# Two moves in the matmul engine's order of a fused attention and feed-forward block

## The reference, cut to what matters

```python
x = x + tanh(g_xattn) * attention(layernorm(x), ctx, ctx, mask, Wq, bq, Wk, bk, Wv, bv, Wo, bo)
x = x + tanh(g_ffn) * ffn(layernorm(x))

def ffn(h):
    h = qat_lora_linear(h, W_fc, b_fc, A_fc, B_fc)          # 256 -> 1024
    h = gelu(h)                                             # exact
    return qat_lora_linear(h, W_proj, b_proj, A_proj, B_proj)   # 1024 -> 256

def qat_lora_linear(x, W, b, A, B):
    scale = max(abs(W)) / 127                               # one scale for the whole matrix
    Wq = clip(round(W / scale), -128, 127) * scale
    return x @ Wq.T + b + 2.0 * (x @ A.T) @ B.T             # rank 16
```

## Time and profile before

| | |
|---|---|
| median of 3 runs | 204.48 us (203.13 to 204.89) |
| profiled execution | 204.89 us, span from first to last instruction 202.9 us |
| PE, PEld | 187.9 us (93%), 140.4 us (69%) |
| DVE | 145.4 us (72%) |
| ACT, POOL | 107.2 us (53%), 108.2 us (53%) |
| mean granted TensorE clock | 0.98 of full |

### The profile page before, as it was taken

The page is one execution under the profiler, slowest core; times in us unless marked ns, Lnnn a source line. Parts: engine busy times, 40 slices in busy tenths (PEclk is TensorE's granted clock), DMA queues, the critical chain, the costliest instruction groups (busy, mean ns, idle before and its releaser), DMA issues.

```text
span 202.9 us, 3501 instructions
## 1 busy us (share of the span) xinstructions
PE 187.9 (93%) x1241; PEld 140.4 (69%) x1241; DVE 145.4 (72%) x295; ACT 107.2 (53%) x187; POOL 108.2 (53%) x145
## 2 busy tenths in 40 slices
PE   6999965999996999999999999999998989999992
PEld 4656832566775976786778856967787748867991
DVE  2869799678289478897568979776479865954724
ACT  3151935784857446665447356643465464236521
POOL 3528979236939548539249662185377640344600
PEclk9999998799999799999999999999999999999998
DMA  6997000000060000000000000000000000010002
GB/s 182 262 251 277 22 0 2 5 0 0 2 210 0 0 0 29 0 27 29 26 0 0 3 0 26 29 26 26 0 2 5 0 29 26 0 52 3 0 0 103
DMA packets 10010, 8.38 MB, mean 41 GB/s; under 512 B 3165, under 2 KB 9722, under 8 KB 9994
## 3 DMA queue, kind: packets, MB, share of 16 engines
q1 hardware_dynamic: 9538, 8.03, 12.4%
q10 hardware_dynamic: 456, 0.14, 0.4%
HBM read 6.07 MB, written 2.10 MB: 40 GB/s over the span
## 4 chain that ended last, share of the span: by engine, by line
PE 72%; POOL 9%; DVE 8%; issue 6%; ACT 4%; DVEq 0%; POOLq 0%
PE ps L1190 13%; PE ps L1170 6%; PE ps L1114 6%; PE ps L1144 6%; PE ps L1103 6%; PE ps L1174 6%; POOL shifted L316 5%; PE ps L987 4%; PE ps L1124 4%; PE ps L1131 4%; PE ps L1212 2%; PE ps L1181 2%; PE ps L978 2%; PE ps L1158 2%; ACT probsT L447 2%
## 5 line engine op out<-in xcount | busy, mean ns | idle before, releaser
L316 POOL TENSOR_TENSOR shifted<-shifted,row_max 128x512 f32<-128x512 f32 x32 | 35.8, 1133 | 17.3 <-DVE row_max L752 17.2
L1190 PE MATMUL ps<-wprojT,h_hi 128*128 128x288 f32 x128 | 37.2, 314 | 1.7 <-ACT wprojT L496 1.7
L803 DVE TENSOR_TENSOR h_lo<-wfc_sb,h_hi 128x512 fp32r<-128x512 f32 x32 | 25.3, 797 | 17.4 <-POOL h_hi L335 17.4
L1190 PE MATMUL ps<-wprojT,h_lo 128*128 128x288 f32 x128 | 35.6, 301 | 0.0
L335 POOL TENSOR_SCALAR h_hi<-wfc_sb 128x512 fp32r<-128x512 f32 x32 | 21.9, 689 | 23.9 <-ACT wfc_sb L632 23.9
L632 ACT ACTIVATE wfc_sb<-ps,bias_cols,wscale 128x512 f32<-128x512 f32 x32 | 24.5, 779 | 18.8 <-PE ps L1181 16.9
L1190 PEld LDWEIGHTS ps<-wprojT,h_hi 128*128 128x128 f32 x128 | 24.9, 195 | 2.8 <-ACT wprojT L496 2.2
L447 ACT ACTIVATE probsT<-ps 128x512 f32<-128x512 f32 x32 | 19.0, 598 | 14.2 <-PE ps L1114 13.9
L739 DVE TENSOR_TENSOR shifted<-ps,mask_neg 128x512 f32<-128x512 f32 x32 | 20.8, 683 | 7.4 <-PE ps L1103 7.2
L1190 PEld LDWEIGHTS ps<-wprojT,h_lo 128*128 128x128 f32 x128 | 24.8, 194 | 0.2
L1114 PE MATMUL ps<-ident,shifted 128*128 128x128 f32 x128 | 20.2, 284 | 4.2 <-POOL shifted L316 4.2
(11 more groups left out here) (154 smaller groups left out, 375.7 us busy)
## 6 DMA issues: line engine op xcount, KB each, us to landing
wfc_sb<-in_L_ffn_W_fc SPq DMA_DIRECT2D x1, 1024.0 KB, 7.6
wproj_sb<-in_L_ffn_W_proj SPq DMA_DIRECT2D x1, 1024.0 KB, 8.9
wproj_sb<-in_x SPq DMA_DIRECT2D x2, 512.0 KB, 3.8
out<-x_front SPq DMA_DIRECT2D x8, 128.0 KB, 1.7
out<-wproj_sb SPq DMA_DIRECT2D x8, 128.0 KB, 1.7
x_front<-in_x SPq DMA_DIRECT2D x2, 256.0 KB, 3.6
x_front<-in_x SPq DMA_DIRECT2D x1, 512.0 KB, 4.6
wk_sb<-in_L_xattn_Wk SPq DMA_DIRECT2D x1, 256.0 KB, 3.9
```

The lines of the kernel that those rows point to most:

```text
L316: nc.gpsimd.tensor_tensor(shifted[:, slot], shifted[:, slot], row_max[:, slot].unsqueeze(2).broadcast_to([P, HH, KC]), ALU.subtract)\
L803: nc.vector.tensor_tensor(h_lo[:, f], hidden[:, f % HIDDEN_SLOTS], h_hi[:, f].bitcast(F32), ALU.subtract).then_inc(h_split, 1)
L1190: last = nc.tensor.matmul(dst[:, 0:DOWN], h[:, f, t * P:(t + 1) * P], wprojT[:, f], start=(f == 0 and n == 0), stop=(f == FC - 1 and n == ...
```

## The change

The transposes of W_proj's first half move from behind up tile 5 to behind up tile 4 (after the lora product of tile 2). ACT reads them behind gelu 5 in place of gelu 6. The scores of the next chunk's second pair leave the loop over up tiles (they stood behind tile 7) and become the first work of `attention_start`, behind the last lora product; in chunk 1's case they also stand behind the wait for the read of W_proj's first half. The scores of the first pair stay behind tile 3. All other queues keep their order.

```diff
-SCORED = (3, 7)
...
-                    if c == 0 and f == 6:
+                    if c == 0 and f == 5:
                         read_wprojT(0)
...
-                    if c == 0 and f == 5:
+                    if c == 0 and f == 4:
                         transpose_wproj(0)
-                    if c < LAST and f in SCORED:
-                        scores(c + 1, SCORED.index(f))
+                    if c < LAST and f == 3:
+                        scores(c + 1, 0)
                     if c == 0 and f == 7:
                         transpose_wproj(1)
...
                 if c == 1:
                     wait_read(pe, ("wprojT", 0))
                     pe.wait_ge(aT_ready, 1)
+                scores(c, 1)
                 down(c - 1, 0, 0)
```

## The result

| | before | after |
|---|---|---|
| median of 10 runs | 204.38 us (202.82 to 205.08) | 201.64 us (200.40 to 203.15) |
| profiled execution | 204.89 us, span 202.9 | 201.03 us, span 199.0 |
| mean granted clock in that execution | 0.98 | 0.996 |

After to before is 0.9881 (by the means, 201.59 to 204.01), with a 95% interval of 0.9834 to 0.9929: faster, by 1.2%. The forecast was 202.3, with 200.8 to 204.1.

The account below looks back on a forecast made before the run. TensorE, busy 93% of the span, was taken as the bound; its wait for W_proj's read cost twice, by length and slow clock. 204.89 - 0.84 - 1.55 = 202.50, or 202.09 against the median; forecast 202.3, range 200.8 to 204.1 us.

Parts of the forecast that it names:

- (a): Chunk 0, up tile 4: moved W_proj transposes cost PE nothing; following POOL and DVE work up to 0.43 us later.
- (b): First boundary: W_proj read behind gelu 5 starts at 61.20, ends 62.21; PE resumes 0.26 us later, at 62.47.
- (c): First boundary: PE's wait 0.92 us in place of 1.75, first down product 0.84 earlier; later boundaries 0.
- (d): Behind the first boundary's wait: the slow clock stretch goes, gain 1.55 us.
- (e): After the first down products: second shift still in time by 0.27 us; bound 0 to 0.44, taken as 0.
- the slower rival: All three boundaries: POOL and DVE contention lengthens two shifts by 0.43 each, 2.6 us in all; 206.6 us, chance 0.06.
- Only the shorter wait counts: First boundary: slow stretch stays, gain only 0.84; 203.6 us against the median, 204.0 against the profiled execution; chance 0.27.
- Both slow stretches go: Boundary's slow stretch and the untouched one at 34 to 38 both absent: 200.9 us, chance 0.15.

Follow-up runs that it names:

- the first kernel with only the other stops filled: Kernel before, unread 128-column matmuls filling PE's four stops in chunk 0's attention, boundary wait unfilled: ratio 0.9985; medians 201.83 us at whole clock, 203.12 with one slow stretch.

## Why the prediction was right

**(a) The transposes moved at no cost: right.** They stand behind lora 2 with no stop (the row has no bracket), and from lora 5 on the boundary has the same order of work as forecast.

```profile
54.99 0.62 PE L1062 MATMUL ps<-ident_bf,probsT 128*128 128x128 bf16 x8
```

One reading under (a) was off: 54.48 is where POOL begins its copies of gelus 0 and 1, two in 1.21 us, so the bank was free near 55.1 and not by 54.48. That was still some 1.2 ahead of the transposes.

**(b) The read behind gelu 5: right, and mis-sized in one term.** Gelu to read is 0.68 again. But PE goes on 0.05 after the read's end (60.89 to 60.94), where 0.26 was taken over from the old profile. With late scores alone it is 0.06 (61.40 to 61.46). Where a down product comes first it is 0.26 before, 0.25 and 0.26 with the wait filled, and 0.35 in the first kernel with only the other stops filled (63.10 to 63.45).

```profile
60.39 1.01 ACT L495 ACTIVATE wprojT<-ps 128x1024 fp32r<-128x1024 bf16 x1
62.09 1.01 ACT L496 ACTIVATE wprojT<-ps 128x1024 fp32r<-128x1024 bf16 x1
```

The first row is of the late scores, the second of that kernel. So the delay goes with what stands first behind the wait; I had put it down to the wait. What in the down product takes the 0.2 to 0.3 was not tried.

**(c) The stop: right.** 0.80 against a forecast of 0.92, and the first down product earlier by 1.03 against 0.84; that difference of 0.19 is the 0.21 of (b) but for 0.02. At the later boundaries the forecast of 0 holds. From the fourth pair's scores of the first boundary to those of the second it was 42.87 before,

```profile
73.08 0.39 PE L1103 MATMUL ps<-k_hi,q_hi 64*128 64x256 f32 x2
...
115.95 0.39 PE L1103 MATMUL ps<-k_hi,q_hi 64*128 64x256 f32 x2
```

and it is 42.86 after (69.17 to 112.03); from the second to the third it was 42.96 (115.95 to 158.91) and is 42.98 (112.03 to 155.01).

```profile
69.17 0.39 PE L1102 MATMUL ps<-k_hi,q_hi 64*128 64x256 f32 x2
...
107.17 0.66 PE L1113 MATMUL ps<-ident,shifted 128*128 128x128 f32 x4 [0.43 <-POOL shifted L315]
...
112.03 0.39 PE L1102 MATMUL ps<-k_hi,q_hi 64*128 64x256 f32 x2
```

The stop of 0.43 for the second shift is that of the earlier trace rows; the rows are of the changed kernel.

**(d) The clock: right in direction and price, wrong as a certainty.** The price, 1.55, was measured as 1.54 in the profiled pair and as 1.3 to 1.4 between the levels of the kernel with its other stops filled. But the forecast took it as lost in every run before and won in every run after. With the other stops filled it was lost in 5 of 12 at this stop, and in 0 of 12 after. The reason given for its going, a stop shorter than the 1.55 at 27.76 that left the clock at 1.00, was weak: stops of 1.5 and 1.84 at the boundary also leave the clock whole in some runs. What the comparison of medians shows, 2.74, is 1.0 of shorter stop, and the rest goes with fewer slow stretches; in the profiled pair one of the two that are gone is that at 34, which the change leaves alone. That the forecast's 2.39 came near is in part luck: the ten runs of before have a median of 204.38, the 75 beside the experiments one of 203.37, only 1.7 above the changed kernel.

**(e) What is late next: right.** No stop for a shift between 60 and 70. The first two shifts there now take 1.42 and 1.47:

```profile
59.86 1.42 POOL L315 TENSOR_TENSOR shifted<-shifted,row_max 128x512 f32<-128x512 f32 x1 [0.21 <-DVE row_max L751]
61.25 1.20 POOL L334 TENSOR_SCALAR h_hi<-wfc_sb 128x512 fp32r<-128x512 f32 x2
62.42 1.47 POOL L315 TENSOR_TENSOR shifted<-shifted,row_max 128x512 f32<-128x512 f32 x1
```

Before they took 1.04 each (the second is in the earlier trace rows). What VectorE did beside them is its split of a hidden tile, first before, then after:

```profile
60.92 1.04 POOL L316 TENSOR_TENSOR shifted<-shifted,row_max 128x512 f32<-128x512 f32 x1
60.99 1.52 DVE L803 TENSOR_TENSOR h_lo<-wfc_sb,h_hi 128x512 fp32r<-128x512 f32 x1 [0.36 <-POOL h_hi L335]
64.83 0.92 DVE L803 TENSOR_TENSOR h_lo<-wfc_sb,h_hi 128x512 fp32r<-128x512 f32 x1
```

```profile
59.69 0.69 DVE L802 TENSOR_TENSOR h_lo<-wfc_sb,h_hi 128x512 fp32r<-128x512 f32 x1
61.90 1.09 DVE L802 TENSOR_TENSOR h_lo<-wfc_sb,h_hi 128x512 fp32r<-128x512 f32 x1 [0.93 <-POOL h_hi L334]
```

Before, the shift began first (60.92 and 64.17) and kept its 1.04, and the split took 1.52 and 0.92; after, the split began first (59.69 and 61.90) with 0.69 and 1.09, and the shift is the longer one. That is what the Trainium skill's rule on the interfaces that POOL and VectorE share (GPSIMD Engine Reference, Specifications) would let one expect, and it was the price of the slower rival. But the second shift ends at 63.89 and PE comes to it at 64.74, a cover of 0.85 where (e) had 0.27: the 0.43 that (a) was to add to its start did not come (3.66 after lora 5, 62.42 less 58.76, where it was 4.07). At the later boundaries the stop for the second shift is 0.44 before and 0.43 after, so the rival's 2.6 us did not appear, and PE's waits for the shift stay at 4.2.

**The rivals.** "Only the shorter wait counts" is right for the runs whose clock was whole before, and gives 1.0 there, where 0.84 was said. "Both slow stretches go" is what the profiled execution after happens to be (201.03, where 200.9 was said), and six runs of ten have a whole clock.

## What to carry to other kernels

Before taking a slow stretch of the clock out of one profile as a cost, count how many executions have it: a stop of PE that lets the clock fall in one run in two is worth half of what the profile shows. Ask of two moves made together which one earns: here the earlier producer did it, and the work moved behind the wait was no help once the read was early (0.4 slower with it than without). Independent work belongs ahead of a wait, where it fills the stop.

## What was not expected of the hardware

The same stop in the same place lets the clock fall in some executions and not in others: 1.84 us in 5 of 12, 1.5 in 1 of 12, 0.80 in none. The three levels of the kernel before, 201.61, 203.33 and 204.98, go with the number of slow stretches that a run's mean clock tells; what decides it from run to run is open.

The shift on POOL took 1.04 or 1.42 to 1.47 us for the same shape at the same boundary. In the rows under (e) the shift takes longer where VectorE's split began ahead of it; no run changed that order alone.
